# Zero-weight matmuls added to TensorE's instruction stream around and inside a bidirectional GRU loop

## The chip, the cores and the metric

The kernel runs on one core of a Trainium2 chip. The metric is the device time of one execution in microseconds, taken as the median of several runs.

## The reference

The input x is 16 images of 32 x 32 positions with 128 channels. Layer normalisation is followed by a small image statistic that decides, image by image, whether positions are read row by row or column by column. The 1024 positions then run through two GRUs, one forward and one backward, hidden size 128, and an output projection is added to x:

```python
def step(h, xt):
    gh = h @ whh.T + bhh
    xr, xz, xn = jnp.split(xt, 3, axis=-1)
    hr, hz, hn = jnp.split(gh, 3, axis=-1)
    r = jax.nn.sigmoid(xr + hr)
    z = jax.nn.sigmoid(xz + hz)
    n = jnp.tanh(xn + r * hn)
    h_new = (1.0 - z) * n + z * h
    return (h_new, h_new)
...
z = seq @ in_w.T + in_b
yf = _gru_dir(z @ gru_wih_f.T + gru_bih_f, gru_whh_f, gru_bhh_f, False)
yb = _gru_dir(z @ gru_wih_b.T + gru_bih_b, gru_whh_b, gru_bhh_b, True)
y = jnp.concatenate([yf, yb], axis=-1) @ out_w.T + out_b
return x + y.reshape(Bx, Hx, Wx, C)
```

The recurrence can't be batched over time: step t + 1 of a direction needs the state of step t.

## The kernel before

**Ahead of the loop.** For each of 16 images VectorE (DVE) takes mean and variance, GpSimd (POOL) and ScalarE (ACT) normalise, TensorE (PE) transposes (L560) and ACT writes both reading orders, `seq` and `big`. The input and gate weights are folded into one matrix, `wcomb`. A chain of small matmuls and DVE operations then decides the reading order (`mask`). PE writes the biases of the first block into PSUM (`fill_bias`, `fill_bias_half`, weights `bias6` on 6 rows, moving operand `ind` of 256 columns), waits for `select_done`, which DVE sets after two selections at L891, and adds the input part with 12 matmul instructions (6 `fill_input`, fp32, two instructions each).

**The loop.** 1024 steps, each with both directions, d = 0 and d = 1. Eight steps are a block; PSUM banks `R`, `Z` and `NX` are double-buffered by block (index q), so that the step in hand reads block q while the next block's banks 1 - q are filled. One step of one direction is this chain:

- PE, L702: nine 128x16 fp16 matmuls, three for each gate. The order is reset gate, candidate's hidden part, update gate. The first three release ACT.
- ACT, L524: sigmoid of the reset gate into `rpair`; L527: sigmoid of the update gate into `gain`; L530: tanh of the candidate into `drive`.
- DVE, L915: a scan that forms the candidate's argument in PSUM from `rpair`; L942: an auxiliary product with the old state; L926: a scan that gives the new state; L935: its split into two fp16 halves, `halves`, which the next step's matmuls read.

All engines work in program order. DVE's order in a step is candidate 0, product 0, (an output addition, L907, in two of eight steps), state 0, candidate 1, split 0, product 1, state 1, split 1. ACT's is reset, update, tanh of d = 0 and then of d = 1.

PE's order in a step (`body`, L719 to L738) is the nine matmuls of d = 0, one bias fill for the next block (six of eight steps; step 4 has `output_bias` instead, step 7 nothing), the nine of d = 1, and then two 128-column fp32 instructions: the output projection in steps 0 and 1, an input fill in steps 2 to 7. In the first block there is no finished block to project, so steps 0 and 1 have nothing after d = 1. I call the place between the nine of d = 0 and the nine of d = 1 the *bias slot*. In the profile the fills and step matmuls all carry L652, the line of the helper `mm`; they are told apart by their tiles.

Of the kernel before, what the change touches and what calls it, by code (L numbers as in the profile page):

```python
# [20 lines left out]
P = 128  # L21
# [20 lines left out]
BF16 = mybir.dt.bfloat16  # L42
# [5 lines left out]
G_R, G_Z, G_N, G_HN = range(4)  # L48
# [71 lines left out]
def build(nc, x, gamma, beta, w1t, b1, w2t, b2, in_w, in_b, wiht, whht, bih, bhh, outwt, out_b, consts, out):  # L120
    ctx = ExitStack()

    def sb(name, shape, dt=F32):
        return ctx.enter_context(nc.sbuf_tensor(name, shape, dt))

    def sem(name):
        return ctx.enter_context(nc.semaphore(name))
# [21 lines left out]
    ind = sb("ind", [6, 2 * P], BF16)  # L149
# [19 lines left out]
    bias_part = sb("bias_part", [P, 9 * 3])  # L169
    bias6 = sb("bias6", [6, 4 * HID], BF16)  # L170
    obias = sb("obias", [3, C], BF16)
    ones3 = sb("ones3", [3, P], BF16)
    mlp1 = sb("mlp1", [4, 32])
    mlpb1 = sb("mlpb1", [32, 1])
# [27 lines left out]
    R, Z = bank[0:2], bank[2:4]  # L202
# [33 lines left out]
    cast_set = sem("cast_set")  # L236
# [310 lines left out]
    def _(pe):  # L547
# [103 lines left out]
        def mm(o, w, m, start=False):  # L651
            return nc.tensor.matmul(o, w, m, start=start, stop=True, skip_group_check=True)  # L652
# [7 lines left out]
        def fill_bias(q, which):  # L660

            bk = (R if which == G_R else Z)[q]
            return mm(bk[:, 0:2 * TB * B], bias6[:, which * HID:(which + 1) * HID], ind[:, :], start=True)
# [8 lines left out]
        def fill_input(q, kblk, g, d):  # L672

            kk = kblk if d == 0 else NBLK - 1 - kblk
            src = seq[:, :, kk * TB:(kk + 1) * TB].rearrange("c b s -> c s b")
            w = wcomb[:, d, g * HID:(g + 1) * HID]
            if g == G_N:
                return mm(nx(q, d)[:, :, :, 1], w, src)
            return mm(gate(R if g == G_R else Z, q)[:, :, d, :], w, src)

        FILL_BIAS = [(fill_bias, G_R), (fill_bias_half, G_HN, 0), (fill_bias, G_Z), (fill_bias_half, G_HN, 1),
                     None, (fill_bias_half, G_N, 0), (fill_bias_half, G_N, 1), None]
        FILL_INPUT = [None, None, (G_R, 0), (G_R, 1), (G_Z, 0), (G_Z, 1), (G_N, 0), (G_N, 1)]
        def project(q, d, start=False):

            h = state[:, d, q * TB:(q + 1) * TB, :].rearrange("p s (b k) -> p (s b) k", k=3)[:, :, 1]
            return mm(Y[q][:, d * C:(d + 1) * C], h, outw[:, d, :], start=start)

        def output_bias(q):  # L690
            return mm(Y[q][:, 0:C], ones3[:, :], obias[:, :])

        def step(base, r, d):

            q, s, e = r // TB, r % TB, r % 2
            low, high = halves[:, 1 - e, d, 0, :], halves[:, 1 - e, d, 1, :]
            at = place(s, d)
            out_of = {G_R: gate(R, q)[:, at, d, :], G_Z: gate(Z, q)[:, at, d, :], G_N: nx(q, d)[:, at, :, 0]}

            def run(g, parts):  # L700
                for k, h in parts:
                    ins = mm(out_of[g], wsplit[:, k, d, g * HID:(g + 1) * HID], h)  # L702
                return ins

            if base + r > 0:
                pe.wait_ge(halves_ready[d], base + r)

            o, others = 1 - d, base + (r + d)
            alone = isinstance(base, int) and base + r + d == 0
            if not alone:  # L710
                pe.wait_ge(reset_and_hn[o], 2 * others)
            parts = ((0, high), (1, high), (2, low))
            run(G_R, parts).then_inc(reset_pre[d], 1)
            run(G_N, parts).then_inc(reset_and_hn[d], 1)
            if not alone:
                pe.wait_ge(update_ready[o], others)
            run(G_Z, parts).then_inc(update_pre[d], 1)

        def body(base, kblk, last=False):  # L719
            for r in range(RING):  # L720
                q, s = r // TB, r % TB
                filling = not (last and q == 1)
                done = kblk + q - 1
                step(base, r, 0)
                if filling and FILL_BIAS[s] is not None:
                    fill, *what = FILL_BIAS[s]
                    fill(1 - q, *what)
                if s == 4 and done >= 0:
                    output_bias(1 - q).then_inc(y_ready, 1)
                step(base, r, 1)  # L730
                if s == 0 and done >= 0:
                    if done > 0:
                        pe.wait_ge(y_used, 2 * done)
                    project(1 - q, 0, start=not filling)
                if s == 1 and done >= 0:
                    project(1 - q, 1)
                if filling and FILL_INPUT[s] is not None:
                    fill_input(1 - q, kblk + (q + 1), *FILL_INPUT[s])  # L738

        pe.wait_ge(bias_rows, 1)  # L740
        pe.wait_ge(cast_set, 2)
        pe.wait_ge(weights_set, 2)
        pe.wait_ge(init_done, N_INIT)
        for g in (G_R, G_Z):
            fill_bias(0, g)
        for g in (G_HN, G_N):
            for d in range(2):
                fill_bias_half(0, g, d)
# [5 lines left out]
        for i in range(L // RING - 1):  # L754
            body(i * RING, i * 2)
        body(L - RING, NBLK - 2, last=True)

        for d in range(2):
# [8 lines left out]
    def _(dve):  # L767
        v = nc.vector
# [6 lines left out]
            dve.wait_ge(link_v, links[0])  # L775

        v.memset(ones3[:, :], 1.0).then_inc(cast_set, 1)
        v.memset(eps[:, :], EPS).then_inc(eps_set, 1)

# [238 lines left out]
```

## Time and profile before

| | |
|---|---|
| runs, median (lowest to highest) | 1676.18 us (1672.85 to 1676.67), 3 runs |
| the profiled execution's own time, and its span | 1678.4 us, 1676.6 us |
| mean granted TensorE clock (1 is 2.4 GHz) | 0.522 |
| busy share PE, PE weight loads, DVE, ACT, POOL | 96%, 72%, 86%, 69%, 3% |
| ahead of the loop, loop, end | 0 to 84.7, 84.7 to 1671, 1671 to 1676.6 us |

A busy share says that an engine had an instruction in hand, not that it sets the time: short matmuls overlap, and each is recorded for some 0.18 us though the next starts long before it ends. What bounds a recurrence is read from the timeline, start by start.

### The profile page before, as it was taken

The numbers are of one execution on the slowest core, as the hardware profiler recorded it, in microseconds if no ns is written. First come the engines' busy times: TensorE is split into PE (matmuls) and PEld (weight loads), VectorE is DVE, ScalarE is ACT, GpSimd is POOL, SyncE is SP. The second block draws the span as 40 slices with busy tenths as digits, with TensorE's granted clock in tenths as the row PEclk, the third lists the DMA queues.
The fourth block names the chain that finished last, engine by engine and source line by source line (L and its number), as shares of the span: only waits on it lengthen the run. The fifth ranks groups of instructions, "written<-read, shape, count | busy, mean of one in ns | idle before, by whom it ended". The sixth has DMA issues, their size and how long they took to land.

```text
span 1676.6 us, 61286 instructions
## 1 busy us (share of the span) xinstructions
PE 1609.8 (96%) x21671; PEld 1203.5 (72%) x21671; DVE 1441.4 (86%) x8900; ACT 1152.9 (69%) x6226; POOL 52.7 (3%) x142
## 2 busy tenths in 40 slices
PE   6799999999999999999999999999999999999997
PEld 3477777777777777777777777777777777777775
DVE  6789999888888888888888888888888888888887
ACT  6766666666666666666666666666666666666666
POOL 6500000000000000000000000000000000000000
PEclk9855555555555555555555555555555555555555
DMA  5200000000000000000000000000000000000000
GB/s 177 77 15 12 12 15 12 14 13 12 15 12 12 15 12 15 12 12 15 12 12 8 13 14 12 13 13 12 15 12 13 13 11 15 12 13 13 11 14 17
DMA packets 40359, 31.28 MB, mean 19 GB/s; under 512 B 3576, under 2 KB 37880, under 8 KB 40056
## 3 DMA queue, kind: packets, MB, share of 16 engines
q1 hardware_dynamic: 40056, 27.35, 5.6%
q8 instruction: 177, 2.90, 0.7%
q14 instruction: 126, 1.03, 0.2%
HBM read 18.95 MB, written 8.39 MB: 16 GB/s over the span
## 4 chain that ended last, share of the span: by engine, by line
DVE 68%; ACT 21%; issue 7%; PE 2%; POOL 1%; DMA 0%; SPq 0%; DVEq 0%; POOLq 0%
DVE state L926 31%; ACT drive L530 21%; DVE bank L915 18%; DVE halves L935 12%; DVE big L907 3%; DVE seq L891 2%; DVE xin L907 1%; POOL xin L401 1%; DVE drive L942 1%; PE bank L560 1%; PE bank L552 1%; DMA gamma_row<-in_gamma 0%; ACT seq L455 0%; PE bank L652 0%; ACT big L460 0%
## 5 line engine op out<-in xcount | busy, mean ns | idle before, releaser
L652 PEld LDWEIGHTS bank<-halves,wsplit 128*128 128x128 f16 x18432 | 648.4, 105 | 396.7 <-DVE halves L935 289.2
L652 PE MATMUL bank<-halves,wsplit 128*128 128x16 f16 x18432 | 834.3, 181 | 39.7 <-DVE halves L935 36.2
L926 DVE TENSOR_TENSOR_SCAN state<-gain,drive 128x48 f32<-128x48 f32 x2048 | 526.7, 257 | 165.2 <-ACT drive L530 15.4
L652 PE MATMUL bank<-seq,wcomb 128*128 128x128 f32 x1536 | 592.9, 482 | 2.9 <-DVE seq L891 2.9
L530 ACT ACTIVATE drive<-bank 128x16 f32<-128x16 f32 x2048 | 395.9, 193 | 267.5 <-DVE bank L915 3.0
L524 ACT ACTIVATE rpair<-bank 128x16 f32<-128x16 f32 x2048 | 380.3, 186 | 225.3 <-PE bank L652 225.3
L915 DVE TENSOR_TENSOR_SCAN bank<-rpair,bank 128x32 f32<-128x32 f32 x2048 | 453.1, 221 | 3.4 <-ACT rpair L524 3.4
L935 DVE SCALAR_TENSOR_TENSOR halves<-state 128x32 f16<-128x32 f32 x2048 | 402.9, 197 | 35.5
L527 ACT ACTIVATE gain<-bank 128x16 f32<-128x16 f32 x2048 | 394.1, 192 | 0.0
L652 PEld LDWEIGHTS bank<-seq,wcomb 128*128 128x128 f32 x1536 | 386.0, 311 | 3.1 <-DVE seq L891 3.1
L942 DVE SCALAR_TENSOR_TENSOR drive<-gain,state 128x16 f32<-128x16 f32 x2046 | 365.8, 179 | 0.0
L652 PE MATMUL bank<-ind,bias 6*128 6x128 bf16 (+1 forms) x768 | 297.2, 388 | 0.0
L652 PE MATMUL bank<-outw,state 128*128 128x128 f32 x512 | 197.9, 491 | 0.9 <-DVE state L926 0.9
L652 PEld LDWEIGHTS bank<-outw,state 128*128 128x128 f32 x512 | 128.7, 310 | 1.0 <-DVE state L926 1.0
L652 PEld LDWEIGHTS bank<-ind,bias 6*128 6x128 bf16 x768 | 75.3, 98 | 18.0
L907 DVE TENSOR_TENSOR big<-bank,big 128x128 f32<-128x128 f32 x192 | 54.5, 284 | 0.0
L401 POOL TENSOR_SCALAR xin<-xin,rstd,shift 128x128 f32<-128x128 f32 x112 | 48.9, 453 | 18.2 <-DVE shift L799 10.4
L891 DVE COPY_PREDICATED seq<-mask,big 128x160 f32<-128x160 int32 (+2 forms) x98 | 38.6, 395 | 0.0
L652 PE MATMUL bank<-obias,ones 3*128 3x128 bf16 x128 | 36.2, 283 | 0.0
L560 PE MATMUL bank<-con,xin 128*128 128x128 f32 x128 | 19.6, 303 | 17.1 <-POOL xin L401 17.1
L560 PEld LDWEIGHTS bank<-con,xin 128*128 128x128 f32 x128 | 16.1, 157 | 26.3 <-issue 14.0
L785 DVE BATCH_NORM_STATS2 stats<-xin 128x6 f32<-128x128 f32 x128 | 26.2, 276 | 5.8 <-DMA xin<-in_x 5.8
(104 smaller groups left out, 186.9 us busy)
## 6 DMA issues: line engine op xcount, KB each, us to landing
xin<-in_x SPq DMA_DIRECT2D x16, 512.0 KB, 3.5
big<-in_x SPq DMA_DIRECT2D x96, 64.0 KB
out<-big SPq DMA_DIRECT2D x96, 64.0 KB
xin<-in_x SPq DMA_DIRECT2D x32, 64.0 KB
out<-xin SPq DMA_DIRECT2D x32, 64.0 KB
wih<-in_wiht SPq DMA_DIRECT2D x2, 384.0 KB, 5.9
con<-in_consts SPq DMA_DIRECT2D x1, 572.0 KB
whh<-in_whht SPq DMA_DIRECT2D x2, 192.0 KB, 7.0
```

The lines of the kernel that those rows point to most:

```text
L401: ins = g.tensor_scalar(xin[:, to, j, :], xin[:, q, j, :], rstd[:, q, j:j + 1], shift[:, q, j:j + 1], ALU.mult, ALU.add)
L524: act.activation(rpair[:, e, 2 * B * d:2 * B * (d + 1)].rearrange("p (n k) -> p n k", k=2)[:, :, 1], R[q][:, at:at + B], ACT.Sigmoid, scal ...
L527: act.activation(thirds_of(gain, e, d)[:, :, 1], Z[q][:, at:at + B], ACT.Sigmoid, scale=negative).then_inc(update_ready[d], 1)
L530: act.activation(thirds_of(drive, e, d)[:, :, 0], candidate_of(q, e, d).rearrange("p (n k) -> p n k", k=2)[:, :, 1], ACT.Tanh, scale=negat ...
L560: ins = nc.tensor.transpose(pair[n % 2][:, j * P:(j + 1) * P], xin[:, xhat_slot(n), j, :], identity)
L652: return nc.tensor.matmul(o, w, m, start=start, stop=True, skip_group_check=True)
L891: return v.copy_predicated(seq[:, :, t0:t1], mask[:, :].unsqueeze(2).to_broadcast([P, B, t1 - t0]), seq_v[:, :, t0:t1])
L907: v.tensor_tensor(t, Y[j % 2][:, d * C:(d + 1) * C], t, ALU.add).then_inc(y_used, 1)
L915: v.tensor_tensor_scan(candidate_of(q, e, d), rpair[:, e, 2 * B * d:2 * B * (d + 1)], NX[q][d][:, at:at + 2 * B], 0.0, ALU.mult, ALU.add). ...
L926: v.tensor_tensor_scan(state[:, d, ring, :], gain[:, e, cols], drive[:, e, cols], 0.0, ALU.mult, ALU.subtract).then_inc(state_ready[d], 1)
L935: v.scalar_tensor_tensor(out=halves[:, e, d, :, :], in0=new[:, :, 2].unsqueeze(1).to_broadcast([P, 2, B]), scalar=-BIG, in1=both, op0=ALU. ...
L942: v.scalar_tensor_tensor(out=thirds_of(drive, e, d)[:, :, 1], in0=thirds_of(gain, e, d)[:, :, 1], scalar=-1.0, in1=old[:, :, 1], op0=ALU.a ...
```

## The change

A tile `nought` of zeros (6 rows, 128 columns, bf16) is set by one more DVE memset, which PE's existing wait on `cast_set` now includes. A helper `keep_busy` multiplies it with the first columns of `ind` and accumulates the zeros into bank `Z`, so no value changes. It is issued

- 14 times with 256 columns, after the first two bias fills and ahead of the other four, before PE waits for `select_done`;
- in the bias slot of every filling step: none in steps 0 to 2, 128 columns in steps 3 to 6, 256 in step 7;
- three times with 256 columns after the nine matmuls of d = 1 in steps 0 and 1 of the first block, where there is no projection (this time into `R`).

```diff
--- before.py
+++ after.py
@@ -169,6 +169,7 @@
     bias_part = sb("bias_part", [P, 9 * 3])
     bias6 = sb("bias6", [6, 4 * HID], BF16)
     obias = sb("obias", [3, C], BF16)
+    nought = sb("nought", [6, P], BF16)
     ones3 = sb("ones3", [3, P], BF16)
     mlp1 = sb("mlp1", [4, 32])
     mlpb1 = sb("mlpb1", [32, 1])
@@ -679,6 +680,11 @@
             return mm(gate(R if g == G_R else Z, q)[:, :, d, :], w, src)
 
 
+        def keep_busy(q, columns):
+
+            mm(Z[q][:, 0:columns], nought[:, :], ind[:, 0:columns])
+
+        KEEP_BUSY = (0, 0, 0, P, P, P, P, 2 * P)
         FILL_BIAS = [(fill_bias, G_R), (fill_bias_half, G_HN, 0), (fill_bias, G_Z), (fill_bias_half, G_HN, 1),
                      None, (fill_bias_half, G_N, 0), (fill_bias_half, G_N, 1), None]
         FILL_INPUT = [None, None, (G_R, 0), (G_R, 1), (G_Z, 0), (G_Z, 1), (G_N, 0), (G_N, 1)]
@@ -725,6 +731,8 @@
                 if filling and FILL_BIAS[s] is not None:
                     fill, *what = FILL_BIAS[s]
                     fill(1 - q, *what)
+                if filling and KEEP_BUSY[s] > 0:
+                    keep_busy(1 - q, KEEP_BUSY[s])
                 if s == 4 and done >= 0:
                     output_bias(1 - q).then_inc(y_ready, 1)
                 step(base, r, 1)
@@ -734,15 +742,20 @@
                     project(1 - q, 0, start=not filling)
                 if s == 1 and done >= 0:
                     project(1 - q, 1)
+                if done < 0 and s < 2:
+                    for k in range(3):
+                        mm(R[1 - q][:, 0:2 * P], nought[:, :], ind[:, :])
                 if filling and FILL_INPUT[s] is not None:
                     fill_input(1 - q, kblk + (q + 1), *FILL_INPUT[s])
 
         pe.wait_ge(bias_rows, 1)
-        pe.wait_ge(cast_set, 2)
+        pe.wait_ge(cast_set, 3)
         pe.wait_ge(weights_set, 2)
         pe.wait_ge(init_done, N_INIT)
-        for g in (G_R, G_Z):
-            fill_bias(0, g)
+        fill_bias(0, G_R)
+        fill_bias(0, G_Z)
+        for k in range(14):
+            keep_busy(0, 2 * P)
         for g in (G_HN, G_N):
             for d in range(2):
                 fill_bias_half(0, g, d)
@@ -775,6 +788,7 @@
             dve.wait_ge(link_v, links[0])
 
         v.memset(ones3[:, :], 1.0).then_inc(cast_set, 1)
+        v.memset(nought[:, :], 0.0).then_inc(cast_set, 1)
         v.memset(eps[:, :], EPS).then_inc(eps_set, 1)
```

## Rows read from the trace of the kernel before

**Rows 1.** The page's part 4, the chain that ended last: by engine, by line.

```profile
DVE 68%; ACT 21%; issue 7%; PE 2%; POOL 1%; DMA 0%; SPq 0%; DVEq 0%; POOLq 0%
DVE state L926 31%; ACT drive L530 21%; DVE bank L915 18%; DVE halves L935 12%; DVE big L907 3%; DVE seq L891 2%; DVE xin L907 1%; POOL xin L401 1%; DVE drive L942 1%; PE bank L560 1%; PE bank L552 1%; DMA gamma_row<-in_gamma 0%; ACT seq L455 0%; PE bank L652 0%; ACT big L460 0%
```

**Rows 2.** Busy time by stretch: start:end, length, engines, granted clock, DMA share, GB/s.

```profile
41.96:65.85 23.89, 19.52 (x79) 7.47 (x79) 19.80 (x140) 20.91 (x31) 18.83 (x44) 1.00 0.41 134
...
72.70:76.10 3.40, 3.40 (x41) 2.45 (x41) 2.82 (x11) 0.45 (x1) 0.00 (x0) 0.50 0.00 0
76.10:79.50 3.40, 2.17 (x28) 1.43 (x26) 2.34 (x8) 2.10 (x4) 0.00 (x0) 1.00 0.00 0
79.50:82.10 2.60, 0.00 (x1) 0.01 (x1) 2.13 (x9) 1.66 (x3) 0.00 (x0) 0.50 0.00 0
82.10:84.70 2.60, 2.60 (x12) 2.60 (x13) 0.00 (x0) 0.00 (x0) 0.00 (x0) 0.50 0.13 38
400.00:800.00 400.00, 391.24 (x5398) 295.79 (x5397) 345.57 (x2133) 276.75 (x1551) 0.00 (x0) 0.50 0.05 13
```

**Rows 3.** Timeline, one step: start us, length us, engine, line, operation, tiles, count.

```profile
801.16 0.41 PE L652 MATMUL bank<-halves,wsplit 128*128 128x16 f16 x9
...
801.44 0.19 ACT L524 ACTIVATE rpair<-bank 128x16 f32<-128x16 f32 x1 [0.21 <-PE bank L652]
...
801.50 0.39 PE L652 MATMUL bank<-ind,bias 6*128 6x128 bf16 x1
...
801.68 0.22 DVE L915 TENSOR_TENSOR_SCAN bank<-rpair,bank 128x32 f32<-128x32 f32 x1
...
801.82 0.41 PE L652 MATMUL bank<-halves,wsplit 128*128 128x16 f16 x9
...
801.93 0.19 ACT L530 ACTIVATE drive<-bank 128x16 f32<-128x16 f32 x1
...
802.10 0.18 ACT L524 ACTIVATE rpair<-bank 128x16 f32<-128x16 f32 x1
802.16 0.26 DVE L926 TENSOR_TENSOR_SCAN state<-gain,drive 128x48 f32<-128x48 f32 x1
...
802.33 0.22 DVE L915 TENSOR_TENSOR_SCAN bank<-rpair,bank 128x32 f32<-128x32 f32 x1
802.46 0.19 DVE L935 SCALAR_TENSOR_TENSOR halves<-state 128x32 f16<-128x32 f32 x1
...
802.58 0.19 ACT L530 ACTIVATE drive<-bank 128x16 f32<-128x16 f32 x1
...
802.71 0.41 PE L652 MATMUL bank<-halves,wsplit 128*128 128x16 f16 x9
802.81 0.26 DVE L926 TENSOR_TENSOR_SCAN state<-gain,drive 128x48 f32<-128x48 f32 x1
802.99 0.19 ACT L524 ACTIVATE rpair<-bank 128x16 f32<-128x16 f32 x1 [0.21 <-PE bank L652]
803.10 0.20 DVE L935 SCALAR_TENSOR_TENSOR halves<-state 128x32 f16<-128x32 f32 x1
...
803.22 0.22 DVE L915 TENSOR_TENSOR_SCAN bank<-rpair,bank 128x32 f32<-128x32 f32 x1
```

**Rows 4.** Timeline: first and last step's reset gate, a late candidate scan, the closing projections.

```profile
85.19 0.19 ACT L524 ACTIVATE rpair<-bank 128x16 f32<-128x16 f32 x1 [4.00 <-PE bank L652]
...
1669.75 0.19 ACT L524 ACTIVATE rpair<-bank 128x16 f32<-128x16 f32 x1 [0.23 <-PE bank L652]
...
1670.63 0.20 DVE L915 TENSOR_TENSOR_SCAN bank<-rpair,bank 128x32 f32<-128x32 f32 x1
...
1671.45 1.19 PE L652 MATMUL bank<-outw,state 128*128 128x128 f32 x4 [0.94 <-DVE state L926]
```

**Rows 5.** Timeline ahead of the loop, fills and the gap before the first step.

```profile
78.42 0.81 PE L652 MATMUL bank<-ind,bias 6*128 6x256 bf16 x6
...
82.10 2.99 PE L652 MATMUL bank<-seq,wcomb 128*128 128x128 f32 x12 [2.87 <-DVE seq L891]
```

## The prediction

> **What bounds the kernel now.** I read the chain that ended last first [rows 1]: 68% of it is DVE, 21% ACT, 2% PE. The state scan L926, the tanh L530 and the candidate scan L915 carry it. A kernel whose TensorE is busy 96% of the time has a chain that hardly touches TensorE; that is the first warning about this change. The second view is the busy time by stretch, for the granted clock [rows 2]: it is 1.00 up to 65.85 us, falls before 72.70, is 1.00 again from 76.10 to 79.50, and 0.50 (1.2 GHz) from then on. The whole loop runs at the low level though its PE is busy 391.24 of 400 us. Before each fall PE had been idle or in short matmuls (2.17 of 3.40 us from 76.10); before the rise it had none of that (3.40 of 3.40 us).
>
> The third view is one step, start by start [rows 3]. The mean step is (1669.75 - 85.19) / 1023 = 1.549 us [rows 4], and three closed loops of work fit it, which is why no single engine explains it:
>
> - *Loop one*, a direction by itself, with PE: first matmul 801.16, reset gate 801.44, candidate 801.68, tanh 801.93, state 802.16, split 802.46, next step's first matmul 802.71. 0.28 + 0.24 + 0.25 + 0.23 + 0.30 + 0.25 = 1.55.
> - *Loop two*, both directions, without PE: candidate 0 at 801.68, tanh 0 801.93, state 0 802.16, candidate 1 802.33, tanh 1 802.58, state 1 802.81, split 1 803.10, candidate 0 of the next step 803.22. 0.25 + 0.23 + 0.17 + 0.25 + 0.23 + 0.29 + 0.12 = 1.54. The 0.17 and the 0.12 are DVE's program order: the operation before is still running (0.26 and 0.20 long) when the next starts. The others are an operation's length and about 0.03 for its semaphore.
> - *Loop three*, over two steps, through the bias slot: first matmul of d = 0 at 801.16 to that of d = 1 at 801.82 (0.66), from there to candidate 0 at 803.22 (1.40), and from a candidate 0 to the first matmul after it (801.68 to 802.71, 1.03). 3.09 for two steps, 1.545 each. The slot is full: the last matmul of the nine starts at 801.16 + 0.41 - 0.17 = 801.40, the bias fill at 801.50, and d = 1 follows 0.32 later. Ahead of the loop six such fills take 0.81 from the first start to the last end at the full clock [rows 5]; less the last one's 0.3, that is 0.10 a fill, so 0.21 at half of it, and the remaining 0.11 is the next weight load.
>
> So a faster TensorE relieves loops one and three, and loop two stays. Loop two is what the change can't buy back.
>
> **Does the clock rise and stay?** Everything hangs on this, and no row decides it. The gap in which the clock was lost is filled: 14 matmuls of 0.10 us from about 78.6 end near 80.1 at the full clock, or of 0.21 near 81.6 at the low one, and either way PE goes into the fills at 82.10 with less than 2 us of idleness instead of 2.87 [rows 5]. For entering the loop at the full clock I am fairly confident. Inside the loop it is less clear. At 2.4 GHz the same columns take half the time, so the array streams for a smaller share of the step than the loop of before does at 1.2 GHz, and that larger share never raised the clock in 1.59 ms [rows 2]. The dense fills at 82.10 to 84.70, 2.60 of 2.60 us, didn't raise it by themselves either. Once lost inside the loop, I take it as lost for good, since the change adds only some 100 columns to a step. What speaks for holding: PE is never out of work for more than about 0.3 us in the loop, whereas both falls came with gaps and tiny matmuls, and from 41.96 to 65.85 the clock held with idle time of 4.4 us in 23.9. I give it 6 in 10.
>
> The Trainium skill (TensorE: Matmul & The Clock Gate, Part 1, "What's actually happening") has the array throttled by default, released by sustained activity and throttled again by idleness. Taken as it stands the loop of before would be at the full clock already, and the change would do nothing but add work; this trace disagrees, with 0.50 beside a busy share of 98%.
>
> **What a held clock is worth.** *Loop one*: the three reset matmuls and their way out take 0.28 at the low clock. No row shows 16-column fp16 matmuls at the full clock. The least is nothing but the last one's columns, under 0.01; the most would be half of the whole 0.28. The gate waits for the end of the array's pipeline, of which the columns are a small part, so I take 0.02 to 0.04: loop one goes to about 1.52. *Loop three*: the fill's 0.21 becomes 0.10 and the added 128 columns cost 0.05 to 0.10, so the slot shrinks or at worst stays: under 1.53. *Loop two*: unchanged at 1.54 by its starts. It has a little give: a candidate scan that starts late behind its data ends in 0.20 instead of 0.22 [rows 4, 3], so one whose data come early may do with 0.20 too; with both candidates at that, 1.50, with one, 1.52, with none, 1.54. The mean of 1.549 holds steps in which loops one and three are the last, and these come down to loop two. I take 1.537, near its starts: 0.012 a step, times 1024 = 12.3 us. The ends: 0.005 (5 us) and 0.024 (25 us).
>
> The single-matmul latency that the Trainium skill gives (same page, "Single matmul latency") is (219 + N) / 1.2 ns at the low and (398 + N) / 2.4 ns at the full clock, 196 and 172 ns for N = 16. By that loop one would go to 1.527, and if it were the only bound the loop would gain some 23 us; no run here shows it yet.
>
> *Entry*: the 12 fp32 instructions after `select_done` take 2.99 us [rows 5], one every 0.23; at the full clock half, so 1.3 us less on the path to the first step. *End*: four such instructions, 1.19 us at 1671.45, on the path [rows 4]: 0.4 less. Sum: 12.3 + 1.3 + 0.4 = 14.0.
>
> **What it costs.** The memset is one more small DVE instruction at the very start, where DVE then waits for the first image: nothing. The wait on `cast_set` is met long before. No DMA and no other queue is touched. The 14 matmuls lie ahead of a wait that ends at 82.1; at the low clock they and the four fills behind them end at 81.6 + 0.8 = 82.4, so they would cost 0.3 us, at the full one nothing. The three of 256 columns in steps 0 and 1 stand where later steps have two fp32 instructions of 0.77 together; at the full clock 0.3, hidden; at the low one 0.64, at most 0.1 late, twice. In the slots: nothing at the full clock, by loop three.
>
> **Sum.** The profiled execution: 1678.4 - 14.0 = 1664.4. It lies 2.2 above the median of the runs, so 1662 for the median (-0.8%).
>
> **The rivals.**
>
> - *The clock falls back in the loop, and the added matmuls lengthen a full slot* (the other side). The slots of steps 3, 5 and 6 hold a bias fill and get 128 columns more: at least 0.105 (half of 0.21), at most another whole fill, 0.21. Steps 4 and 7 only come up to what a bias step has. Loop three passes a slot every second step, so two of the three a block: 2 x 0.105 / 8 = 0.026 a step, 27 us, and 54 at the upper end. It decides from the point at which the clock is lost; lost at once, 1676 + 27 = 1703, or up to 1730. For it: the slot is full by the starts, and the low clock of the loop of before. Against: the entry at the full clock. 0.25.
> - *The clock falls back, and the slot takes the matmul.* If the 0.32 after the bias fill is a wait for the split of d = 1 rather than PE's own work, the first added 0.1 is hidden: 1676, within 5 us. The split at 803.10 ends at 803.30, and matmuls usually follow a split by about 0.05; so the two bounds are close and I can't exclude it. 0.12.
> - *The clock holds and PE's part of loop one was the real bound*, loop two giving way with it (0.17 and 0.12 shrink, because DVE's next operation starts earlier when its data are there). 0.023 to 0.03 a step: 24 to 31 us and the 1.7 of entry and end: 1645 to 1650. Against: the chain has 2% PE. 0.08.
> - *The clock holds and nothing moves*, loop two at 1.545: 1674. 0.05.
>
> **How the numbers follow.** The forecast, clock held and loop two the bound, has 0.50, with its own range 1655 to 1670. A measurement of this kernel can tell some 0.3% (5 us) from no change. Faster: nearly all of 0.50 and the 0.08, less the thin end: 0.55. Same: 0.12, the 0.05 and a little: 0.19. Slower: the 0.25 and a part-held clock: 0.26. To leave out no more than 2 in 10 the range must take in the lower half of the slower case and most of the faster one: 1650 to 1706.
>
> **What would show it.** In the trace of after: the granted clock of the loop's stretches, 1.00 or 0.50. If 1.00: the reset gate starts 0.24 to 0.26 after the first matmul instead of 0.28; candidate 0 to candidate 0 reads 1.53 to 1.54, with 0.17 after state 0 and 0.12 after split 1 as now; ACT's reset gates wait less for PE, and the difference is found as waiting ahead of the candidates; the 12 fp32 instructions take 1.5 us. If 0.50: in steps 3, 5 and 6 the nine of d = 1 start 0.76 or more after those of d = 0. The prediction is wrong if the clock holds and the step falls below 1.52 (then loop two is no floor), or if it holds and the step doesn't shorten (then loop two was the bound by itself already).

## The result: 38 us slower, and the clock stays low

| | before | after |
|---|---|---|
| median of the runs | 1674.75 us | 1713.05 us (1712.78 to 1714.12) |
| ratio, 95% interval | | 1.0227 (1.0214 to 1.0239) |
| span of the profiled execution | 1676.6 us | 1712.3 us |
| mean granted TensorE clock | 0.522 | 0.521 |

The median of before is over four runs now, and so differs from the 1676.18 us of three above. One more run of the kernel before, of the 19 taken beside the first comparisons below, took 2312.93 us at a granted clock of 1.00; it is left out of the ratios, has no trace, and its cause is open.

The forecast was 1662 us and a clock that holds. The time is that of the rival on the other side (1703 to 1730), and lies outside the range (1650 to 1706). The page of after, its span and its parts 1 and 4:

```profile
span 1712.3 us, 62597 instructions
...
PE 1683.8 (98%) x22326; PEld 1229.4 (72%) x22326; DVE 1466.0 (86%) x8901; ACT 1160.5 (68%) x6226; POOL 53.4 (3%) x142
...
DVE 68%; ACT 21%; issue 7%; PE 2%; POOL 1%; DMA 0%; SPq 0%; DVEq 0%; POOLq 0%
```

The shares of the chain are those of before to the digit [rows 1]. A chain that says DVE 68% doesn't tell why each turn of it has become longer; the granted clock and the timeline do. Busy time by stretch of after, for [rows 2]:

```profile
72.70:76.40 3.70, 2.88 (x35) 2.14 (x34) 2.43 (x9) 2.40 (x5) 0.00 (x0) 0.95 0.00 0
76.50:78.00 1.50, 1.50 (x8) 0.88 (x6) 1.29 (x8) 1.26 (x2) 0.00 (x0) 0.50 0.00 0
78.70:81.20 2.50, 2.50 (x11) 2.50 (x12) 0.00 (x0) 0.00 (x0) 0.00 (x0) 0.50 0.14 41
81.25:88.00 6.75, 6.75 (x89) 4.44 (x88) 5.39 (x31) 4.06 (x23) 0.00 (x0) 0.50 0.09 25
400.00:800.00 400.00, 399.85 (x5422) 294.98 (x5419) 343.20 (x2080) 272.03 (x1514) 0.00 (x0) 0.50 0.05 13
```

The clock was lost between 76.4 and 76.5 us, in the middle of the 14 added matmuls. PE then was busy without a gap in 76.50 to 78.00 and in all of the fills, and still entered the loop at 0.50 and stayed there. Now one step of after, number 5 of its block, against [rows 3]:

```profile
801.07 0.41 PE L653 MATMUL bank<-halves,wsplit 128*128 128x16 f16 x9
...
801.35 0.19 ACT L525 ACTIVATE rpair<-bank 128x16 f32<-128x16 f32 x1 [0.22 <-PE bank L653]
...
801.41 0.39 PE L653 MATMUL bank<-ind,bias 6*128 6x128 bf16 x1
...
801.51 0.39 PE L653 MATMUL bank<-ind,nought 6*128 6x128 bf16 x1
...
801.84 0.41 PE L653 MATMUL bank<-halves,wsplit 128*128 128x16 f16 x9
...
802.10 0.77 PE L653 MATMUL bank<-seq,wcomb 128*128 128x128 f32 x2
802.12 0.19 ACT L525 ACTIVATE rpair<-bank 128x16 f32<-128x16 f32 x1
...
802.34 0.23 DVE L929 TENSOR_TENSOR_SCAN bank<-rpair,bank 128x32 f32<-128x32 f32 x1
802.47 0.18 DVE L949 SCALAR_TENSOR_TENSOR halves<-state 128x32 f16<-128x32 f32 x1
...
802.71 0.25 PE L653 MATMUL bank<-halves,wsplit 128*128 128x16 f16 x3
```

The nine of d = 0 start at 801.07, those of d = 1 at 801.84: 0.77 where it was 0.66. The zero matmul stands between the bias fill (801.41) and them. From there: the reset gate of d = 1 at 802.12, candidate 1 at 802.34, split 0 behind it at 802.47, the next step at 802.71 (the view ends within its nine matmuls). 0.77 + 0.28 + 0.22 + 0.13 + 0.24 = 1.64 for the step, against 0.66 + 0.28 + 0.23 + 0.13 + 0.25 = 1.55 by [rows 3]. First and last step's reset gate of after, for [rows 4]:

```profile
81.75 0.19 ACT L525 ACTIVATE rpair<-bank 128x16 f32<-128x16 f32 x1 [3.97 <-PE bank L653]
...
1705.64 0.19 ACT L525 ACTIVATE rpair<-bank 128x16 f32<-128x16 f32 x1 [0.23 <-PE bank L653]
```

(1705.64 - 81.75) / 1023 = 1.587 us a step, 0.038 more than the 1.549 of before, times 1024 = 39 us: all of the loss lies in the loop. The spans of these two executions differ by only 35.7 us, since the first step of after began 3.4 us earlier. The change isn't the reason for that: in the traces of this document the first reset gate comes anywhere from 81.20 to 85.19 us, at 81.48 in a run with no work ahead of the loop and at 85.05 in one with it.

Which steps have become longer can be read from the starts of the reset gates of d = 0 over the whole trace, averaged by place in the block. Steps 3, 5 and 6, those with a bias fill and a zero matmul in one slot, take 1.639, 1.643 and 1.640 us; the other five take 1.545 to 1.569. In before all eight take 1.543 to 1.555.

### The profile page after: what moved, and what is told of

Read it like the earlier page. It is cut to its first block, busy times and chain, and to the rows that moved or that the text cites. A ratio compares the mean times of both kernels' runs of the same rounds, so it can differ in the third digit from the quotient of the medians.

```text
span 1712.3 us, 62597 instructions
## 1 busy us (share of the span) xinstructions
PE 1683.8 (98%) x22326; PEld 1229.4 (72%) x22326; DVE 1466.0 (86%) x8901; ACT 1160.5 (68%) x6226; POOL 53.4 (3%) x142
## 4 chain that ended last, share of the span: by engine, by line
DVE 68%; ACT 21%; issue 7%; PE 2%; POOL 1%; DMA 0%; SPq 0%; DVEq 0%; POOLq 0%
DVE state L940 30%; ACT drive L531 20%; DVE bank L929 19%; DVE halves L949 12%; DVE big L921 3%; DVE seq L905 2%; DVE xin L921 1%; POOL xin L402 1%; DVE drive L956 1%; PE bank L653 0%; PE bank L561 0%; PE bank L553 0%; ACT seq L456 0%; DMA gamma_row<-in_gamma 0%; ACT big L461 0%
## 5 line engine op out<-in xcount | busy, mean ns | idle before, releaser
L949 DVE SCALAR_TENSOR_TENSOR halves<-state 128x32 f16<-128x32 f32 x2048 | 396.1, 193 | 35.5
L653 PE MATMUL bank<-ind,nought 6*128 6x128 bf16 (+1 forms) x655 | 237.5, 367 | 0.0
L653 PEld LDWEIGHTS bank<-ind,nought 6*128 6x128 bf16 x655 | 68.7, 105 | 6.4
L561 PE MATMUL bank<-con,xin 128*128 128x128 f32 x128 | 18.2, 287 | 16.7 <-POOL xin L402 16.6
```

The lines of the kernel that those rows point to most:

```text
L561: ins = nc.tensor.transpose(pair[n % 2][:, j * P:(j + 1) * P], xin[:, xhat_slot(n), j, :], identity)
L949: v.scalar_tensor_tensor(out=halves[:, e, d, :, :], in0=new[:, :, 2].unsqueeze(1).to_broadcast([P, 2, B]), scalar=-BIG, in1=both, op0=ALU. ...
```

## The experiments

Each ratio is to the kernel before, run on the same chip, with its 95% interval. The first group asks which part costs and the second what a high clock is worth; the third asks what it takes to hold it. Lines left out of an edit are marked with three dots.

### Which part costs

**Only the slots.** The changed kernel without the work ahead of the loop and in the first two steps:

```diff
-        for k in range(14):
-            keep_busy(0, 2 * P)
...
-                if done < 0 and s < 2:
-                    for k in range(3):
-                        mm(R[1 - q][:, 0:2 * P], nought[:, :], ind[:, :])
```

> Only the added matmuls in the bias slots are kept; the 14 ahead and the three in steps 0 and 1 are gone. Theory (the full slots of steps 3, 5 and 6 lengthen three steps of eight at the low clock): 1712 us, all of the 38 us, and granted clock 0.50 in the loop. Rival (the work ahead of the loop delays it, or shifts the phase of the two directions): under 1690.

Measured: 1712.4 us, 1.0232 (1.0215 to 1.0249). All of the loss.

**Only the work ahead.** The reverse:

```diff
-        KEEP_BUSY = (0, 0, 0, P, P, P, P, 2 * P)
+        KEEP_BUSY = (0, 0, 0, 0, 0, 0, 0, 0)
```

> The reverse: 14 ahead and three in steps 0 and 1, nothing in the slots. Theory: 1675 us, as before, within 2; granted clock 0.50 in the loop. Rival (work ahead is what costs): over 1690. If the fill of the gap were enough for a high clock in the loop, the clock would show 1.00 and the time lie near 1662.

Measured: 1676.8 us, 1.0013 (1.0004 to 1.0023), clock 0.50 in the loop. By the ratio some 2 us (0.7 to 3.8), and filling the gap doesn't give the loop a high clock. The trace shows none of the 2 us: the first reset gate starts at 85.05 (85.19 before) and the loop from there to the last one takes 1584.97 us (1584.56 before). Where they go stays open.

**Without the full slots.**

```diff
-        KEEP_BUSY = (0, 0, 0, P, P, P, P, 2 * P)
+        KEEP_BUSY = (0, 0, 0, 0, P, 0, 0, 2 * P)
```

> The change with the added matmul taken out of steps 3, 5 and 6 and kept in steps 4 and 7, whose slots hold no bias fill. Theory: 1675 to 1680 us, since 128 columns beside the output bias, or 256 alone, only bring the slot to what a bias step has. Rival (any added matmul costs, by contention or issue, in proportion to the number): 2 of 5 matmuls, 3 of 6 units of 128 columns, so 1690 to 1694.

Measured: 1678.1 us, 1.0015 (1.0006 to 1.0025). Half of the added columns in the slots, with the work ahead still in, cost 2.5 us by the ratio, less than a tenth of the loss, so neither issue nor contention in proportion to the work is the cause: it is where the matmul stands. In the trace the loop is 3.3 us longer than that of before, and the slots of steps 4 and 7 read 0.665 from gate to gate in place of 0.65, so these slots weren't quite free.

**Two neighbouring full slots.** The kernel before with 128 zero columns in steps 5 and 6 (the work ahead of the loop is left out too):

```diff
-        KEEP_BUSY = (0, 0, 0, P, P, P, P, 2 * P)
+        KEEP_BUSY = (0, 0, 0, 0, 0, P, P, 0)
```

> The kernel before with 128 zero columns in the slots of steps 5 and 6 alone, which follow each other. By the prediction's loop three, which passes a slot every second step, only one of the two pays: 0.1 x 128 = 13 us, 1687. By a loop of one step through the slot (d = 0, slot, d = 1, its reset gate, candidate 1, split 0 behind it on VectorE, d = 0 of the next step) both pay: 2 x 0.1 x 128 = 25 us, 1699 to 1701.

Measured: 1701.9 us against 1675.9, 1.0153 (1.0135 to 1.0172): 26 us, both pay: in the trace steps 5 and 6 take 1.642 and 1.640 us, and no other step over 1.566. The prediction's two-step loop three is not what carries the delay; the one-step loop through candidate 1 and split 0 is.

**The slot emptied.** The kernel before without its bias fills in the loop; `base is None` is never true (gates wrong from the second block on):

```diff
-                if filling and FILL_BIAS[s] is not None:
+                if base is None and FILL_BIAS[s] is not None:
```

> The kernel before with the bias fills of the loop left out, so that the gates of every block after the first are wrong; only the slot's effect is asked. Theory (at the low clock the full slot is one of the bounds, loop two just under it): the step falls to loop two or loop one, 1.54 us: 1665 to 1672. If the slot is no bound in the kernel before: 1675, no change.

Measured: 1669.5 us, 0.9969 (0.9957 to 0.9980). The full slot was a bound already, worth 5 us: there was no room for the change's matmuls, and little behind it. By the trace every step now takes 1.541 to 1.546 us.

### What a high clock is worth

The kernels from here on use zero weights on all 128 rows (fp16, moving operand from `wsplit`), into the unused half of bank `Z`, a fixed number in every step. The 14 ahead of the loop and the three in each of the first two steps stay, in the same form, unless said otherwise. "One and two" means one of 256 columns in the bias slot and two after the nine of d = 1. The edit, with the pair of numbers (here 1, 2):

```diff
-    nought = sb("nought", [6, P], BF16)
+    nought = sb("nought", [P, P], F16)
...
-            mm(Z[q][:, 0:columns], nought[:, :], ind[:, 0:columns])
+            mm(Z[q][:, 2 * P:2 * P + columns], nought[:, :], wsplit[:, 0, 0, 0:columns])
...
-        KEEP_BUSY = (0, 0, 0, P, P, P, P, 2 * P)
+        KEEP_BUSY = (1, 2)
...
-                if filling and KEEP_BUSY[s] > 0:
-                    keep_busy(1 - q, KEEP_BUSY[s])
+                for k in range(KEEP_BUSY[0]):
+                    keep_busy(1 - q, 2 * P)
...
+                for k in range(KEEP_BUSY[1]):
+                    keep_busy(1 - q, 2 * P)
```

**One and three**, `KEEP_BUSY = (1, 3)`:

> A kernel made to hold the clock: in every step one zero matmul of 256 columns (128 rows) in the bias slot and three after the nine of d = 1, beside the 14 ahead. If the clock stays at 0.50, PE is the bound: 0.21 more in the slot and 0.64 after d = 1, some 2.3 us a step, 2300 us or more. If it rises to 1.00, the same work takes half, and loop two's floor can be read: a step of 1.53 to 1.54 us by the forecast, 1655 to 1670 us in all, if the slot's 0.10 more stays hidden; if the forecast's rival held (PE's part of loop one the real bound), 1.52 and 1645 to 1650.

Measured: 1741.8 us, 1.0403 (1.0385 to 1.0422), mean clock 0.995. **None and three**, `KEEP_BUSY = (0, 3)`:

> As the heavy kernel, but with nothing added in the bias slot: three of 256 columns after d = 1 in every step. At 1.00: 1655 to 1670 us (loop two) or 1645 to 1650 (PE's part the bound). At 0.50: 0.64 more after d = 1, less some 0.05 of room: about 2.1 us a step, 2200 us.

Measured: 1707.6 us, 1.0197 (1.0179 to 1.0215), mean clock 0.992. The clock held nearly throughout and both were slower, which neither expectation had. The timeline of the second, PE:

```profile
800.74 0.37 PE L653 MATMUL bank<-halves,wsplit 128*128 128x16 f16 x9
800.97 0.49 PE L653 MATMUL bank<-wsplit,nought 128*128 128x256 f16 x3
801.29 0.60 PE L653 MATMUL bank<-seq,wcomb 128*128 128x128 f32 x2
801.71 0.39 PE L653 MATMUL bank<-halves,wsplit 128*128 128x16 f16 x9
```

The last of the nine starts at about 800.74 + 0.37 - 0.17 = 800.94, and the next step's first matmul at 801.71, 0.77 later; in [rows 3] it is 802.71 - (801.82 + 0.41 - 0.17) = 0.65. The pair of fp32 instructions takes 0.60 at the full clock against 0.77 in the timeline of after (802.10) at the low one, not half, so three zero matmuls beside it overfill this place. Both expectations took the pair as halved.

**One and two**, all real work kept:

> One zero matmul of 256 columns in the bias slot and two after d = 1, in every step: all real work kept. If the clock holds: after d = 1 0.22 + 0.40 fits 0.65, the bias slot costs some 0.05, 1.57 to 1.60 a step, 1700 to 1730 us. If it holds only in part, between that and 2100.

Measured: **1657.5 us, 0.9888 (0.9872 to 0.9905), mean clock 0.993**. Faster than both kernels, and than the 1700 to 1730 us expected: the slot costs nothing at the high clock. Its loop by stretch, and one step:

```profile
100.00:1600.00 1500.00, 1484.04 (x23396) 1097.35 (x23393) 1317.92 (x8171) 1014.09 (x5879) 0.00 (x0) 1.00 0.05 13
```

```profile
799.91 0.39 PE L653 MATMUL bank<-halves,wsplit 128*128 128x16 f16 x9
...
800.41 0.22 DVE L931 TENSOR_TENSOR_SCAN bank<-rpair,bank 128x32 f32<-128x32 f32 x1
...
800.56 0.37 PE L653 MATMUL bank<-halves,wsplit 128*128 128x16 f16 x9
800.66 0.19 ACT L531 ACTIVATE drive<-bank 128x16 f32<-128x16 f32 x1
...
800.82 0.19 ACT L525 ACTIVATE rpair<-bank 128x16 f32<-128x16 f32 x1
800.89 0.26 DVE L942 TENSOR_TENSOR_SCAN state<-gain,drive 128x48 f32<-128x48 f32 x1
...
801.06 0.20 DVE L931 TENSOR_TENSOR_SCAN bank<-rpair,bank 128x32 f32<-128x32 f32 x1
801.18 0.20 DVE L951 SCALAR_TENSOR_TENSOR halves<-state 128x32 f16<-128x32 f32 x1
...
801.30 0.19 ACT L531 ACTIVATE drive<-bank 128x16 f32<-128x16 f32 x1
...
801.44 0.38 PE L653 MATMUL bank<-halves,wsplit 128*128 128x16 f16 x9
801.53 0.26 DVE L942 TENSOR_TENSOR_SCAN state<-gain,drive 128x48 f32<-128x48 f32 x1
...
801.71 0.19 ACT L525 ACTIVATE rpair<-bank 128x16 f32<-128x16 f32 x1 [0.21 <-PE bank L653]
801.82 0.20 DVE L951 SCALAR_TENSOR_TENSOR halves<-state 128x32 f16<-128x32 f32 x1
...
801.94 0.22 DVE L931 TENSOR_TENSOR_SCAN bank<-rpair,bank 128x32 f32<-128x32 f32 x1
```

The prediction's loop two, start by start: candidate 0 at 800.41, tanh 800.66, state 0 800.89, candidate 1 801.06, tanh 801.30, state 1 801.53, split 1 801.82, candidate 0 801.94. 0.25 + 0.23 + 0.17 + 0.24 + 0.23 + 0.29 + 0.12 = 1.53. The 0.17 and the 0.12, DVE's order, are as in [rows 3]; by these starts the one thing that gave was candidate 1 (0.20 long in place of 0.22). The reset gate starts 0.27 after the first matmul (801.44 to 801.71) in place of 0.28. The starts are rounded to 0.01; averaged over the steps from 400 to 900 us the way is 0.284 in before and 0.266 here. The slot: the nine of d = 0 at 799.91, those of d = 1 at 800.56, 0.65 with a bias fill and 256 more columns in it.

**Nearly nothing but the recurrence, at either clock.** The kernel before without bias fills (as in the run before), input fills and projections in the loop. The output bias of step 4 stays in the slot:

```diff
-                if filling and FILL_INPUT[s] is not None:
+                if base is None and FILL_INPUT[s] is not None:
...
-                    project(1 - q, 0, start=not filling)
-                if s == 1 and done >= 0:
-                    project(1 - q, 1)
```

> The kernel before with the loop's bias fills, input fills and projections left out, nothing added; the gates and the output of later blocks are wrong, only time is asked. Granted clock 0.50. PE has only the nine matmuls to do, so what is left is loops one and two at the low clock: 1.54 a step, 1664 to 1670 us, like the run without bias fills.

Measured: 1670.9 us, 0.9974 (0.9965 to 0.9984), clock 0.521. The same with `KEEP_BUSY = (2, 4)`, and with the work ahead of the loop:

> The same with zero matmuls of 256 columns on 128 rows in place of what was left out, two in the bias slot and four after d = 1, all of which fit the slots at the full clock (0.22 and 0.43 us). Granted clock 1.00. It shows the step that the two serial loops allow at the full clock with no slot in the way. Loop two as floor: 1.53 to 1.54 a step, 1655 to 1668 us; PE's part of loop one as the real bound: 1.51 to 1.52, 1640 to 1650; no gain from the clock at all: as the bare kernel at the low clock.

Measured: 1665.0 us, 0.9934 (0.9917 to 0.9950), clock 0.997. So without nearly all of PE's side work the low clock gains 5 us, the same as without the bias fills alone, and the high clock some 6 more. The one-and-two kernel, with all its real work, is faster still by 7.5. The trace says why. This is a step 4 of the bare kernel at the high clock, PE:

```profile
802.49 0.38 PE L653 MATMUL bank<-halves,wsplit 128*128 128x16 f16 x9
802.73 0.38 PE L653 MATMUL bank<-wsplit,nought 128*128 128x256 f16 x2
803.04 0.23 PE L653 MATMUL bank<-obias,ones 3*128 3x128 bf16 x1
803.19 0.38 PE L653 MATMUL bank<-halves,wsplit 128*128 128x16 f16 x9
```

Two zero matmuls and the output bias stand in one slot, and the nine of d = 1 start 0.70 after those of d = 0. Steps 4 and 5 take 1.567 and 1.557 us on average and the other six 1.528 to 1.536, as all eight do in the one-and-two kernel (1.528 to 1.535). The excess of the two, (0.036 + 0.026) / 8 x 1024 = 8 us, is the 7.5. The expectation had missed the output bias.

The steps without such a delay compare the two clocks where no slot is in the way: 1.542 us on average at the low one (seven of eight; step 0 takes 1.563, and why wasn't followed up) against 1.531 (six of eight) at the high one, some 11 us over the loop. From 400 to 900 us the bare kernel at the low clock has candidate 0 start 0.218 after its reset gate and 0.127 after split 1, the one-and-two kernel 0.227 and 0.119. So at the low clock the reset gate comes last there (loop one), and at the high clock DVE's own order does (loop two). Candidate 1 is 0.20 long in both, so its shorter time is not what the clock bought in these two.

### What it takes to hold the clock

**The change's own amounts on 128 rows** (the work ahead of the loop and in the first two steps too).

```diff
-    nought = sb("nought", [6, P], BF16)
+    nought = sb("nought", [P, P], F16)
...
-            mm(Z[q][:, 0:columns], nought[:, :], ind[:, 0:columns])
+            mm(Z[q][:, 0:columns], nought[:, :], wsplit[:, 0, 0, 0:columns])
```

> The change with zero weights on 128 rows in place of 6, moving operand an fp16 tile on 128 rows; the same count and columns. 
```profile
78.00:82.20 4.20, 4.20 (x34) 3.64 (x34) 0.72 (x5) 0.81 (x5) 0.00 (x0) 0.50 0.23 65
82.20:85.60 3.40, 3.12 (x47) 1.75 (x45) 3.14 (x21) 2.24 (x14) 0.00 (x0) 1.00 0.00 1
85.60:89.00 3.40, 3.26 (x51) 2.55 (x52) 3.12 (x20) 2.19 (x13) 0.00 (x0) 0.50 0.00 0
```

It was 0.50 through the fills ahead of the loop, 1.00 from 82.2 through the second and third step, and fell at 85.6 after PE had been busy for 3.12 of 3.40 us. Rows alone don't do it at these amounts.

**One and one**, `KEEP_BUSY = (1, 1)`:

> One of 256 columns in each of the two places in every step, between the change and the heavy kernels: shows how much is wanted. At 0.50: the slot grows by 0.21 in six steps of eight and by less in two, and the place after d = 1 by 0.15: 1.85 to 1.95 us a step, 1950 to 2050 us. At 1.00: 1655 to 1670.

Measured: 1886.3 us, 1.1260 (1.1238 to 1.1281), mean clock 0.53: high for single moments, low for the rest, and then PE is the bound (busy 1197.40 us of the 1200 from 400 to 1600). That is less than the 1950 to 2050 us expected for the low clock.

**High first, then the change.** One and two for the first eight loop bodies, the change's amounts after:

```diff
-                if filling and KEEP_BUSY[s] > 0:
+                if base < 8 * RING:
+                    stream(1 - q, 1)
+                elif filling and KEEP_BUSY[s] > 0:
                     keep_busy(1 - q, KEEP_BUSY[s])
...
+                if base < 8 * RING:
+                    stream(1 - q, 2)
```

> The first 8 loop bodies (128 steps, about 200 us) stream one and two zero matmuls of 256 columns a step, which holds the full clock, and from there on the change's own amounts. If the change only failed to enter the loop at the full clock, the clock stays 1.00 to the end: 1655 to 1662 us. If its amounts can't keep a high clock, it falls shortly after step 128 and stays at 0.50: the first eighth near 1.53 a step, the rest at the change's 1.585: 1703 to 1709.

Measured: 1708.7 us, 1.0187 (1.0132 to 1.0241). By stretch:

```profile
100.00:280.00 180.00, 178.22 (x2746) 132.07 (x2744) 167.87 (x1033) 119.03 (x690) 0.00 (x0) 0.96 0.05 13
280.00:300.00 20.00, 19.74 (x287) 14.34 (x287) 17.84 (x111) 13.52 (x77) 0.00 (x0) 0.74 0.03 9
300.00:400.00 100.00, 100.00 (x1359) 73.99 (x1357) 85.47 (x519) 68.02 (x378) 0.00 (x0) 0.50 0.05 13
400.00:1600.00 1200.00, 1200.00 (x16253) 888.55 (x16253) 1027.05 (x6237) 816.07 (x4536) 0.00 (x0) 0.50 0.05 13
```

The loop begins at 0.50 (85 to 115 us), and the stronger stream raises the clock to 1.00 from 116 us on. Its last matmuls start at 286.55; the clock is 0.96 from 285 to 290, 0.50 from 290 on, and doesn't come back. So the entry alone wasn't the fault: the change's amounts can't keep the high clock where it is given to them.

**The stream thinned in the slot.** One and two, but the one in steps 4 and 7 only:

```diff
-                for k in range(KEEP_BUSY[0]):
+                for k in range(KEEP_BUSY[0] if s in (4, 7) else 0):
```

> The one-and-two kernel with the one in the bias slot only in steps 4 and 7, which have no bias fill. If the clock holds: 1655 to 1658 us, as the slot has room for it at the full clock anyway. If it doesn't hold: 0.3 us more after d = 1 at the low clock, over 1900.

Measured: 1832.6 us, 1.0898 (1.0821 to 1.0975), mean clock 0.682, between the two cases expected. It goes up and down:

```profile
85.20:98.70 13.50, 12.96 (x209) 9.02 (x207) 12.34 (x77) 9.05 (x53) 0.00 (x0) 1.00 0.04 10
98.80:108.90 10.10, 10.10 (x130) 7.76 (x130) 8.77 (x52) 5.91 (x34) 0.00 (x0) 0.50 0.01 2
```

The Trainium skill (TensorE: Matmul & The Clock Gate, "HAM oscillation — how this bites in real kernels") describes a clock that swings with the gaps between matmul bursts; here it swings with PE busy 12.96 of 13.50 us, so the busy share doesn't show it coming.

**Six rows or 128.** The one-and-two kernel with the change's tile and operand:

```diff
-    nought = sb("nought", [P, P], F16)
+    nought = sb("nought", [6, P], BF16)
...
-            mm(Z[q][:, 2 * P:2 * P + columns], nought[:, :], wsplit[:, 0, 0, 0:columns])
+            mm(Z[q][:, 2 * P:2 * P + columns], nought[:, :], ind[:, 0:columns])
```

> The one-and-two kernel with its zero matmuls on 6 rows (bf16) in place of 128 rows, the same columns. If rows are nothing to the clock: clock near 1.00 and 1655 to 1662 us. If streams on few rows don't count: clock 0.50, PE-bound, 2000 us or more.

Measured: 2464.5 us, 1.4699 (1.4623 to 1.4774), mean clock 0.514:

```profile
400.00:1600.00 1200.00, 1200.00 (x12333) 712.91 (x12333) 771.03 (x4261) 561.31 (x3100) 0.00 (x0) 0.50 0.03 9
```

PE is busy for all of 1200 us and the clock stays low. Rows, type and operand differ between this and the one-and-two kernel, so two more part them. Six rows, fp16, the same data:

```diff
-    nought = sb("nought", [P, P], F16)
+    nought = sb("nought", [6, P], F16)
...
-            mm(Z[q][:, 2 * P:2 * P + columns], nought[:, :], wsplit[:, 0, 0, 0:columns])
+            mm(Z[q][:, 2 * P:2 * P + columns], nought[:, :], wsplit[0:6, 0, 0, 0:columns])
```

> The one-and-two kernel on 6 rows, but fp16 and with the first six rows of the same moving operand as the 128-row form. If the number of rows decides: granted clock 0.50 in the loop and over 2000 us. If the type or the data decide: 1.00 and 1655 to 1662.

Measured: 2464.7 us, 1.4720 (1.4689 to 1.4751), clock 0.515. And 128 rows with zeros as the moving operand too:

```diff
-    nought = sb("nought", [P, P], F16)
+    nought = sb("nought", [P, 3 * P], F16)
...
-            mm(Z[q][:, 2 * P:2 * P + columns], nought[:, :], wsplit[:, 0, 0, 0:columns])
+            mm(Z[q][:, 2 * P:2 * P + columns], nought[:, 0:P], nought[:, P:P + columns])
```

> The one-and-two kernel on 128 rows with zeros as the moving operand too, so nothing in the array changes. If the number of rows decides: granted clock 1.00 and 1655 to 1662 us. If values in motion decide: 0.50 and over 1900.

Measured: 1656.8 us, 0.9882 (0.9865 to 0.9898), clock 0.993. The rows decide, and the data don't. The type makes no difference on 6 rows; bf16 on 128 rows, and numbers of rows between 6 and 128, weren't run.

**Without the work ahead.** The one-and-two kernel without the 14 and the three of the first steps:

> The one-and-two kernel without anything added ahead of the loop or in the first block's first two steps beyond its one and two. If the loop's own stream raises the clock: the same time within 3 us of the one-and-two kernel, 1655 to 1660. If the work ahead is needed: clock 0.50, over 2000.

Measured: 1657.8 us, 0.9893 (0.9842 to 0.9944), mean clock 0.989. The loop's own stream raises the clock by itself, here between 95 and 100 us, some 15 us into the loop. The 14 matmuls aren't needed for it.

## Why the prediction was wrong, point by point

- **The step that failed: "Does the clock rise and stay?", 6 in 10.** It doesn't. Both halves were wrong. I was "fairly confident" of the entry at the full clock, and in the profile of after the loop was entered at 0.50; and the loop's amounts don't hold it even where it is high already (high first, then the change). I had seen the two facts that spoke for this, the larger share of streaming that never raised the clock in 1.59 ms and the dense fills that didn't, and let "PE is never out of work for more than about 0.3 us" outweigh them. Idle time was the wrong measure: with six rows in the one-and-two kernel PE has none (1200.00 of 1200.00 us) at 0.50, and with 128 it idles for 16 of 1500 us at 1.00.
- **Why it doesn't hold: rows and amounts.** I didn't weigh the rows at all. The zero matmuls use 6 of 128 rows, and even the larger streams on 6 rows left the clock low (2464.5 and 2464.7 us against 1657.5 and 1656.8). With full rows the change's amounts are still too small (1713.8).
- **What a held clock is worth** was right in mechanism and near in size: forecast 14 us and 1662, own range 1655 to 1670; the one-and-two kernel has 18.5 less than before, 1657.5. Loop two was foreseen at 1.537 and is 1.53, with the "little give" of one candidate scan. Loop one was foreseen at 1.52 (reset gate after 0.24 to 0.26); the way is 0.266 on average, so it came down to 1.53 and not below loop two. What moved the step is not the candidate scan's give alone: at the low clock the slot came last, and with the slot emptied loop one, and the high clock relieved both. By the latency formulas of the Trainium skill (TensorE: Matmul & The Clock Gate, "Single matmul latency") the reset path should lose 0.02, an estimate for one matmul of 16 columns; the averages of the traces, 0.284 and 0.266, agree.
- **The entry** was mis-sized: I had the 12 fp32 instructions halved, for 1.3 us. In the one-and-two kernel they run at the high clock and take 2.87 us, against 2.99 [rows 5]: 0.1 us. The loop's 12.3 us was 18.2 in the profiled execution (1566.41 us from the first to the last reset gate, 1584.56 before), so the two errors lean against each other in the sum. The end's 0.4 us was not put to the test, and why these instructions don't halve wasn't traced. The granted clock over the 12, and the 12, in the one-and-two kernel:

```profile
81.50:85.00 3.50, 3.50 (x26) 2.94 (x24) 0.06 (x1) 0.34 (x2) 0.00 (x0) 1.00 0.24 72
```

```profile
81.69 2.87 PE L653 MATMUL bank<-seq,wcomb 128*128 128x128 f32 x12
```

- **The price of the low-clock case** was 27 us, with 54 as its upper end; it is 38. The 0.105 a slot was right (0.66 became 0.77 where I wrote 0.76 or more), the path was not: loop three passes a slot every second step, so I charged two of three. The profile held a shorter loop that I didn't read out, through one slot, the reset gate of d = 1, candidate 1, split 0 waiting behind it in DVE's order, and the next step of d = 0, and it charges every full slot. The two neighbouring slots show it, 26 us and not 13, and so do the 1.64 us of steps 3, 5 and 6 in the trace of after. With it the case would have been 1674.75 + 40. The short price is also why the range ended at 1706, below the time measured.
- **The second rival** (the slot takes the matmul) is out, by the slots-only run. That the slot was full was right, and the run without bias fills puts 5 us on it.
- **Costs of the rest**: "nothing" for memset and waits, up to 0.3 and 0.2 us for the work ahead; measured some 2 us for the work ahead by the ratio (0.7 to 3.8), more than I had, and its trace doesn't show where.

## What to carry to other kernels

A serial loop over several engines has many closed paths of nearly one length, so a place on an engine that "has time" is full as soon as it lies on one of them: go through every path that returns to itself within one step, each engine's program order among its edges, before pricing an insertion. Don't take a busy share for the activity that frees TensorE's clock: make a kernel that streams more than can be wanted, see whether the clock holds and what it is worth, and then thin it until it falls. And work added to hold a clock must fit at the low clock or hold it surely; in between it costs more than it can bring (1713 to 2465 us here, for a gain of 18).

## What was unexpected of the hardware

- Zero matmuls on 6 rows left the granted clock at 0.50 for the whole loop with PE busy 1200.00 of 1200.00 us; the same number and columns on 128 rows held 1.00, also with zeros as moving operand.
- The pair of fp32 instructions with 128 columns took 0.60 us at the full clock and 0.77 at the low one; the nine fp16 matmuls 0.37 to 0.39 against 0.41. A clock twice as fast took 0.018 off the way from the first of them to the reset gate (0.284 to 0.266 on average), and 0.12 off twelve fp32 instructions in a row (2.99 to 2.87).
- One zero matmul of 256 columns in six steps of eight parts a clock that holds for 1.5 ms (1657.5 us) from one that swings (1832.6 us).
